# Moving a router's small steps and a store within the expert stage of a two-layer fused kernel

## The reference, cut to what matters

```python
x = x + _L0_xattn_ref(_layernorm(x), ctx, ctx, mask0, ...)
x = x + _L0_ffn_ref(_layernorm(x), w_red, wg, W1, b1, W2, b2)      # 8 experts, C=256, H=512
    logits = (x @ w_red) @ wg_n.T
    scores, idx = max(softmax(logits)), argmax(softmax(logits))
    h = gelu(x @ W1[idx] + b1[idx]);  o = (h @ W2[idx] + b2[idx]) * scores
x = x + _L1_xattn_ref(_layernorm(x), ctx, ctx, mask1, ...)
x = x + _L1_ffn_ref(_layernorm(x), ...)                              # shared expert + top 2 of 7
```

## Time and profile before

| | us |
|---|---|
| median of 3 runs | 498.2 (498.06 to 504.58) |
| the profiled execution's own time | 498.2 |
| its span, first to last instruction | 496.9 |
| outside the span | 1.3 |

### The profile page before, as it was taken

The page is one execution under the profiler, slowest core; times in us unless marked ns, Lnnn a source line. Parts: engine busy times, 40 slices in busy tenths (PEclk is TensorE's granted clock), DMA queues, the critical chain, the costliest instruction groups (busy, mean ns, idle before and its releaser), DMA issues.

```text
span 496.9 us, 8815 instructions
## 1 busy us (share of the span) xinstructions
PE 480.8 (97%) x3292; PEld 363.1 (73%) x3292; DVE 257.0 (52%) x756; ACT 193.2 (39%) x409; POOL 103.1 (21%) x156
## 2 busy tenths in 40 slices
PE   7899999999999999999999999999999999999995
PEld 6555555568999987554654355657999999999994
DVE  5788887765474655966679465403322222222210
ACT  3517465443556443547466633101222222222221
POOL 6568500012032100300000000650112212122122
PEclk9999999999999999999999999999999999999999
DMA  8650039993132200470000210573897676776712
GB/s 271 202 151 2 2 111 369 373 337 128 44 116 79 84 32 22 159 255 1 2 0 1 75 54 1 186 232 121 273 343 249 195 260 197 221 241 194 255 21 30
DMA packets 43897, 73.14 MB, mean 147 GB/s; under 512 B 3554, under 2 KB 34242, under 8 KB 43845
## 3 DMA queue, kind: packets, MB, share of 16 engines
q1 hardware_dynamic: 34596, 59.95, 36.7%
q0 software_dynamic: 4336, 6.75, 6.0%
q10 hardware_dynamic: 4912, 5.78, 3.5%
HBM read 56.35 MB, written 14.51 MB: 143 GB/s over the span
## 4 chain that ended last, share of the span: by engine, by line
PE 81%; DVE 11%; DMA 3%; issue 2%; ACT 1%; POOL 1%; SPq 0%; ACTq 0%; POOLq 0%; DVEq 0%
PE PS L2067 19%; PE PS L2084 9%; PE PS L939 8%; PE PS L1975 8%; PE PS L1848 6%; PE PS L1861 6%; PE PS L949 6%; DVE W L1148 4%; PE PS L1986 4%; PE PS L970 4%; PE PS L408 3%; PE PS L382 2%; PE PS L958 1%; PE PS L387 1%; PE PS L393 1%
## 5 line engine op out<-in xcount | busy, mean ns | idle before, releaser
L1148 DVE TENSOR_REDUCE W<-PS 128x2 f32<-128x512 f32 x128 | 83.4, 686 | 32.2 <-PE PS L939 31.6
L2067 PE MATMUL PS<-PR,W 128*128 128x128 f32 x836 | 96.6, 275 | 0.0
L2067 PEld LDWEIGHTS PS<-PR,W 128*128 128x128 f32 x836 | 95.1, 192 | 0.1
L939 PE MATMUL PS<-W 32*128 32x256 f32 x512 | 81.0, 399 | 2.8 <-DVE W L1148 1.5
L949 PE MATMUL PS<-W 32*128 32x512 f32 x256 | 76.8, 638 | 0.2
L939 PEld LDWEIGHTS PS<-W 32*128 32x128 f32 x512 | 54.0, 184 | 25.2 <-issue 12.9
L2882 POOL DMA_INDIRECT out<-PR,slots x19 | 29.6, 1559 | 132.8 <-ACT PR L2829 115.8
L2084 PE MATMUL PS<-W,PR 128*128 x228 | 52.4, 379 | 0.0
L1299 ACT ACTIVATE PR<-PS 128x512 f32<-128x512 f32 x64 | 35.0, 595 | 33.0 <-PE PS L949 32.8
L2084 PEld LDWEIGHTS PS<-W,PR 128*128 128x128 f32 x228 | 41.9, 190 | 4.9
L2106 DVE TENSOR_TENSOR PR<-PR,PS 128x512 f32<-128x512 f32 x19 | 13.1, 689 | 58.8 <-PE PS L2067 58.8
(11 more groups left out here) (286 smaller groups left out, 613.0 us busy)
## 6 DMA issues: line engine op xcount, KB each, us to landing
W<-in_rguT SPq DMA_DIRECT2D x19, 1408.0 KB, 6.3
W<-in_L_ffn_W SPq DMA_DIRECT2D x16, 512.0 KB, 9.4
W<-in_rdT SPq DMA_DIRECT2D x5, 768.0 KB, 10.0
scratch_rows<-W SPq DMA_DIRECT2D x1, 2860.0 KB
VR<-scratch_rows SPq DMA_DIRECT2D x19, 130.0 KB
scratch_x<-W SPq DMA_DIRECT2D x1, 2048.0 KB, 14.1
PR<-scratch_x SPq DMA_DIRECT2D x16, 128.0 KB, 2.1
scratch_y<-PR SPq DMA_DIRECT2D x16, 128.0 KB
```

What stands on the lines that cost most here:

```text
L939: m = pe.matmul(PS[:, bank, q * FK:(q + 1) * FK], QT[r:r + 32, g, c:c + 128], KT[r:r + 32, g, b * FK:(b + 1) * FK], start=True, stop=True)
L1148: dve.tensor_reduce(NM[:, s % 2, q:q + 2, c], PS[:, m_bank(use), :].rearrange("p (q n) -> p q n", q=2), AX, ALU.max).then_inc(sem("m_free" ...
L2067: m = pe.matmul(PS[:, bank, j * 128:(j + 1) * 128], W[:, o:o + 128], XS[:, r % 2, k, :], start=(k == 0), stop=(k == 1))
```

## The change

In tile 3's step TensorE issues the strips of logits between `up(3)` and `down(2)` and not in the middle of `up(3)`, their transpose in the middle of `down(2)` and not ahead of it, and the ranks in the middle of `up(4)` and not behind `down(2)`. VectorE has `take_x(5)` between the choice of the expert and the places. At step 11 VectorE does the whole of `combined_statistics` and the two normalised row tiles, which stood behind `take_x(13)` at step 12. SP issues at each step the store of tile i-1 and then the load of tile i+3; it was the other way round.

```diff
@@ combined_statistics
             dve.bn_stats(ST[:, COLUMN["x1_0"] + t, :], X[:, t, :]).then_inc(*v.up())
-        yield
         yield from deviations(v, "x1_0")
@@ ffn0_sp
         for i in tiles:
+            if i > first:
+                store_y(i - 1)
             if i + 3 <= last:
                 load_x(i + 3)
-            if i > first:
-                store_y(i - 1)
         store_y(last)
@@ fast_pe: mid(i)
             if i == 3:
-                pe.wait_ge(sem("lg"), 2)
-                logits_turned(5).then_inc(sem("logits_ps"), 1)
+                taken(6, "rows0_1")
+                taken(7, "rows0_1")
+                logits_strips(0, 4, 5).then_inc(sem("logits_ps"), 1)
@@ fast_pe: first_maxima(i, part), the half hook
-            if (i, part) == (3, "up"):
-                taken(6, "rows0_1")
-                taken(7, "rows0_1")
-                logits_strips(0, 4, 5).then_inc(sem("logits_ps"), 1)
+            if (i, part) == (2, "down"):
+                pe.wait_ge(sem("lg"), 2)
+                logits_turned(5).then_inc(sem("logits_ps"), 1)
+            elif (i, part) == (4, "up"):
+                ranks_pe(1).then_inc(sem("ranks"), 1)
@@ fast_pe: beside(i)
-            elif i == 3:
-                ranks_pe(1).then_inc(sem("ranks"), 1)
@@ fast_dve: beside(i)
         second_rows = statistics(v, "rows0_1", rows_of(1))
-        x1_begun = combined_statistics(v)
...
                 whole(choose_experts(v, 1))
+            elif i == 4:
                 dve.wait_ge(sem("ranks"), 2)
                 whole(places0(v, 1, (sem("ranked"), 2)))
...
             elif i == 11:
                 dve.wait_ge(sem("kept"), 16)
-                next(x1_begun)
-            elif i == 12:
-                whole(x1_begun)
+                whole(combined_statistics(v))
                 for j in range(2):
                     normal_dve("x1_0", j, OB[:, 0, j, :], X[:, j, :]).then_inc(sem("x1_rows"), 1)
+            elif i == 12:
                 dve_xt("x1_0", 0)
```

## The result

| | before | changed |
|---|---|---|
| median of 20 executions each, us | 498.88 (497.52 to 504.58) | 502.16 (499.28 to 504.54) |
| ratio, 95% interval | | 1.0052 (1.0028 to 1.0078) |
| the profiled execution's own time | 498.2 | 502.15 |
| its span | 496.9 | 500.8 |
| its mean granted clock | 0.998 | 0.994 |

By the interval of the ratio the change costs 1.4 to 3.9 us, 2.6 in the middle; the two medians are 3.3 apart. It was forecast as 0.9, and the measured median lies above the forecast's range. The changed kernel's page begins with

A forecast was written before the change was run, and what follows sets the result against it. The prediction took TensorE's instruction stream to bound the kernel, so only its waits count. It added 0.18 us for the loads, net of tile 3's gain, and 0.71 at tile 14 to 498.2, giving 499.1, range 498.0 to 500.9.

The forecast's parts named there:

- steps 11 to 13: At `turn_x(14)` TensorE waits for `take_x(13)`, now behind `deviations` and two normalised row tiles: 0.71 us lost, ends 0.3 and 1.0.
- the lost time lasts: Behind 173 us everything is tied to TensorE, so its stops cost themselves, no clock, and aren't made up.
- no slower: Rival at `turn_x(14)`: `take_x(13)` is done in time or the stop is made up later; 498.1 us, chance 0.15.
- tile 3's step: Strips after all of `up(3)` save a 0.09 us wait for `XT`; nothing waits, and the places come 1.02 later.
- store ahead of load: On SP each load goes a 3.84 us step later; only tile 8 waits, net 0.18 us, ends -0.19 and +0.28.
- The tightest ordinary one: Tile 10's load, issued at 152.69, is seen at 154.92, ahead of `turn_x(10)` at 155.52: 0.60 us to spare.
- the loads set the pace: Rival at tiles 7 to 14: landings over 2.7 us make every second load a wait; 503.1 us, chance 0.07.
- tile 8: Its load goes at 144.91, behind the late `take_y(4)`, and is seen at 147.14, so TensorE is 0.18 us later.
- ScalarE's stop moves: Rival: the 3.25 us idle before tile 5's gelu grows by 1 us (500.1, chance 0.1) or goes (498.8, 0.05).

The follow-up runs named there:

- Experiment 9: Changed kernel with the load again ahead of the store and `take_x(13)` between the deviations and the normalised rows; tile 0's `turn_x` to L958 79.66 us.
- the third profile: Changed kernel, unchanged, profiled a third time in one execution; 503.15 us.
- experiment 5: Kernel before, unchanged, built and run again as a control; median 498.94 us, ratio 0.9987.
- the first profile: Changed kernel as first measured and profiled; the profiled execution took 502.15 us.
- experiment 8: Changed kernel with steps 11 to 13 as before and the load ahead of the store but held until the store's `y_out`; median 499.72 us, ratio 0.9992.
- experiment 4: Kernel before with only the edits to the router's steps in tiles 3 and 4; median 501.01 us, ratio 1.0028.
- experiment 6: Changed kernel, unchanged, run a second time; median 501.68 us, ratio 1.0025.

## Why the prediction was right and wrong

**Right: steps 11 to 13.** 0.71 was forecast, 0.66 to 0.67 measured in each of four profiles, with `take_x(13)` behind the L475 and the bracket on VectorE's copy, as written. The 0.05 is the handover: 0.21 was taken from L1321 to L408, and from `take_x(13)`'s end to the transposes it is 0.15. Experiment 9, with one execution, shows nothing else in this edit that has a price.

**Right: the lost time lasts.** From tile 14 to L958 no profile made anything up, so the rival "no slower" fell. Nor did the clock fall within the stage in any of them.

**Right but for the gain: tile 3's step.** Strips, transpose and ranks wait for nothing, and the places are 1.12 later (136.69 - 135.57; 1.02 forecast). The gain of 0.09 was -0.05, and its reading was wrong: the 0.09 ahead of the strips was no wait for `XT`. In the changed kernel `XT` is ready 1.2 ahead of the strips (L1320 ends at 132.91), and yet `up(3)` takes 134.12 - 132.24 = 1.88 up to them, 0.10 more than twice the 0.89 of half an `up`. So it goes with the change to the narrow strips and moved along. The way back costs 0.10 in `down(2)`, as forecast. The ranks now stand in the middle of `up(4)`, whose second half takes 0.97 instead of 0.89, and the 0.04 that they cost `turn_x(5)` before is saved. I counted the moved instructions and not the kinds of matmul beside them.

**Wrong: the loads, by the landing of 2.1.** The term "store ahead of load" was mis-sized: I took 0.18 net, and it is 0.86 in the mean, between 0.03 and 1.57. Two steps of its working failed.

- *"The time from a load's issue until it lands is 1.8 to 2.2, median 2.1."* The same line of the changed kernel reads

```profile
DMA to landing us min/median/max: 2.1/2.1/3.9
```

and in the third profile 3.7. The median is where it was. The tail is no doing of the change: it was in the kernel before and not to be seen in the earlier trace rows, whose line doesn't cover all 16 loads. Asked load by load, that trace has no landing for six of them, those issued at 126.72, 136.16, 144.91, 152.69, 160.75 and 168.90. The one at 136.16 has its last packet 2.4 after the issue, with a packet of code beside it; with the 0.3 that lie between the last packet and the landing where both are known, that is 2.7. In the control (experiment 5, the kernel before again) the line says it outright:

```profile
DMA to landing us min/median/max: 2.0/2.2/3.4
```

There the load of tile 7 landed 3.3 after its issue and that of tile 9 3.4. Both had a whole step to spare, so TensorE didn't wait.

- *"The tightest ordinary one"*, with 0.60 to spare. The margins were right, 0.6 at the least and none for tile 8. The edit took 3.84 from every load's margin and left it smaller than that tail. In the rival "the loads set the pace" I had the right threshold (a landing over 2.7) but asked for it at every second load, and gave it 0.07. What happens lies between: none to three late loads in each of the seven profiles with the store first. Not even the margin of 1.5 at tile 12 was enough: in the first profile its load (issued at 163.17) met GpSimd's gathers on the same engines, and TensorE started 4.00 later.

**Wrong in part: tile 8.** The issue came out as forecast (1.81 to 1.95 behind `turn_x(7)` where ScalarE is late, against 144.91 - 143.12 = 1.79), and by the landing of 2.1 it would have cost the 0.2 to 0.3 that I gave it. The landing was 2.6 to 2.95 there, with a packet of code on the load's first packets; the scatter's traffic, which I named in the rival, was over. The rival "ScalarE's stop moves" turned out true in the direction that costs less: `take_y(4)` is early in five of thirteen profiles, and then tile 8 is in time, as that rival's 0.05 had it. It was too sure to take one position as the rule. The stop of 3.25 itself, ahead of the gelu, came in the first profile of before alone; in the seven other late ones the gelu is in time and `take_y(4)` idles for 1.5 to 1.6 instead of 0.6 to 0.7. With tile 3's edits the late position was seen in 7 of 9 profiles, without them in 1 of 4. Whether they favour it, and what ScalarE stops for, remains open. So does what tile 8 would do with the store first, ScalarE late and the early scatter: no profile fell so.

**Missing: the clock.** The forecast stood on one execution: the profiled one, 498.2, was also the median of three, and the median of 20 is 0.7 higher. The third of the three, 504.58, was a sign that single executions spread by 6 us, and the range had "some tenths between executions". The clock alone moved the mean of a set of executions by most of a microsecond. By the stretches, 498.9 + 1.6 = 500.5 would have been in the range, and by the times at equal clock, 498.9 + 1.9 = 500.8, just so; with the clock's 0.9 it wasn't. Whether the change makes the lower clock more frequent, this study leaves open. For chance: the places lie ahead of the changed code in most profiles, they differ between profiles of one kernel, and 0.0017 +/- 0.0013 between before and the variants (0.0014 with experiment 8's kernel) is little more than its interval. Against: experiment 4, which waits nowhere, had 0.9912 as well, and the control had the highest mean of all sets, 0.9943.

## What to carry to other kernels

A prefetch whose margin is cut from a step to some tenths of a microsecond is no longer priced by its median landing: ask for the latest last packet of every load, also of those for which nobody waited, and leave room for the tail. With the store first, two to five of twelve loads came 0.5 to 1.8 us behind the median (where the trace has no landing, by the last packet and 0.3), and each profile had none to three for which TensorE waited. An engine that hands tiles to the bounding engine has to make its handover first and its own preparations behind it, by single instructions: here two of them in front cost their 0.7 us in full. And where a change is worth less than about 1% of the time, compare marks inside the stage over several profiles rather than whole times, and the mean clock of every set beside them.

## What the runs showed of the hardware that was not expected

- Instruction code is loaded over the same 16 DMA engines as the data, in single packets of 8 or 16 KB. In the first profile one of 16 KB held one engine for 1.0 us (4.4% of 1.4 us x 16), and the load of 128 KB that it met landed 3.9 after its issue and not 2.1. An 8 KB packet came at 2.85 to 3.10 behind `turn_x(7)` in six executions, so whether the load met it hung on some tenths of its issue.
- The Trainium skill (DMA: Bandwidth & Descriptors, Anatomy of one DMA) has a fixed part of about 2.0 us and the bytes at 436 GB/s, a fit for transfers issued from GpSimd, from which 2.3 was estimated for these loads of SP's. Here an undisturbed load took 2.1, and the disturbed ones 2.6 to 3.9.
- The granted clock falls to 0.50, the level of 1.2 GHz, for 3.4 or 6.8 us at varying places. TensorE had been busy for 4.34 of the 4.80 us ahead of one such fall (experiment 6), and just so in an execution whose clock stayed at 1.00 there. No edit or wait of this study was seen to decide where. A mean clock lower by 0.01 costs 4.3 us in an execution of 499.
- A stop of TensorE at the transposes costs 0.16 to 0.17 more than its bracket of idle time shows (0.81 with 0.64, 0.66 with 0.49, 1.05 with 0.88), and behind a late load the next step takes another 0.05 to 0.06. Time lost at a wait is read from the starts around it.
- Going from full matmuls to strips of 32 columns or back costs about 0.1 us each way (`up(3)` 1.88 instead of 1.78, half a `down` 0.97 instead of 0.87).
